# Second attention: other TensorE work behind the odd units, unread products beside the transposes

## The reference

```python
def _L1_xattn_ref(q, k, v, gamma):
    B, Dq, Lq = q.shape            # 32, 64, 256
    h = N_HEAD                     # 8 heads of 8 rows each
    qh = q.reshape(B, h, dq, Lq)
    kh = k.reshape(B, h, dq, Lk)
    vh = v.reshape(B, h, dv, Lk)
    qk = jnp.einsum('bhdq,bhdl->bhql', qh, kh) * scale
    sm = jax.nn.softmax(qk, axis=-1)
    ret = jnp.einsum('bhql,bhdl->bhdq', sm, vh)
    return gamma * ret.reshape(B, Dv, Lq)

x = x + jnp.tanh(g_xattn[1]) * _L1_xattn_ref(_layernorm(x, axis=-1), ctx_2048, ctx_2048, L1_xattn_gamma)
```

## Time and profile before

| | |
|---|---|
| median of 3 runs | 708.63 us (707.4 to 709.66) |
| the profiled execution's own time | 710.47 us |
| its span, first to last instruction | 708.7 us |
| TensorE busy, whole span | 626.2 us (88%) |
| VectorE, ScalarE, POOL busy | 501.0, 422.5, 283.4 us |
| mean granted clock of TensorE | 0.942 |

### The profile page before, as it was taken

The page is one execution under the profiler, slowest core; times in us unless marked ns, Lnnn a source line. Parts: engine busy times, 40 slices in busy tenths (PEclk is TensorE's granted clock), DMA queues, the critical chain, the costliest instruction groups (busy, mean ns, idle before and its releaser), DMA issues. The chain is left out here.

```text
span 708.7 us, 16712 instructions
## 1 busy us (share of the span) xinstructions
PE 626.2 (88%) x5047; PEld 456.8 (64%) x5047; DVE 501.0 (71%) x885; ACT 422.5 (60%) x859; POOL 283.4 (40%) x385
## 2 busy tenths in 40 slices
PE   3788869999999758999999999999859889999995
PEld 2676747788888655444444444444457779999874
DVE  3878784788887965788888888788427744444656
ACT  3888864434343513888888888888825325555430
POOL 2455544222223453444434443453243624214254
PEclk9999987999999965999999999999959979999998
DMA  5444449000000043344333443342000236546444
GB/s 157 113 111 127 132 141 324 19 1 1 0 0 21 4 137 107 96 114 129 112 104 107 122 118 108 101 120 60 2 0 33 93 103 193 162 128 193 120 135 126
DMA packets 70369, 70.42 MB, mean 99 GB/s; under 512 B 10420, under 2 KB 66580, under 8 KB 70324
## 3 DMA queue, kind: packets, MB, share of 16 engines
q1 hardware_dynamic: 65092, 55.55, 26.7%
q0 software_dynamic: 5232, 14.29, 6.7%
HBM read 38.22 MB, written 31.33 MB: 98 GB/s over the span
## 5 line engine op out<-in xcount | busy, mean ns | idle before, releaser
L1375 DVE TENSOR_REDUCE a_smax<-a_s 128x4 f32<-128x1024 f32 x128 | 153.7, 1208 | 38.9 <-PE a_s L1307 37.6
L1189 ACT ACTIVATE a_prob<-a_st 128x512 f32<-128x512 f32 x256 | 144.1, 596 | 38.8 <-PE a_st L1302 37.5
L1302 PEld LDWEIGHTS a_st<-qop,kop 25*128 25x128 f32 x512 | 60.9, 185 | 71.3 <-issue 54.8
L1307 PE MATMUL a_s<-kop,qop 24*128 24x256 f32 x512 | 99.9, 339 | 7.4 <-DVE a_smax L1375 5.0
L1302 PE MATMUL a_st<-qop,kop 25*128 25x256 f32 x512 | 100.3, 330 | 6.6 <-ACT a_prob L1189 5.7
L1246 PE MATMUL a_pv<-a_prob,a_vt 128*32 128x256 f32 x1024 | 81.6, 391 | 2.2 <-ACT a_pv_sb L1174 0.7
L806 POOL TENSOR_TENSOR f_hs_lo<-f_kept,f_hs_hi 128x512 fp32r<-128x512 f32 x32 | 41.3, 1323 | 89.1 <-ACT f_hs_hi L756 89.1
L1307 PEld LDWEIGHTS a_s<-kop,qop 24*128 24x128 f32 x512 | 60.3, 190 | 9.8 <-DVE a_smax L1375 6.3
L1820 POOL DMA_INDIRECT sorted_rows<-m_xn,m_slot x32 | 32.9, 1029 | 49.5 <-PE m_gu L126 26.7
L124 PE MATMUL f_bank<-f_xt_hi,w_hi 128*128 128x512 f32 x128 | 51.6, 403 | 1.1 <-DVE w_raw L849 0.6
L125 PE MATMUL f_bank<-f_xt_lo,w_hi 128*128 128x512 f32 x128 | 50.8, 397 | 0.0
(11 more groups left out here) (260 smaller groups left out, 1700.7 us busy)
## 6 DMA issues: line engine op xcount, KB each, us to landing
kop<-kop_rows SPq DMA_DIRECT2D x128, 48.0 KB
qop<-qop_rows SPq DMA_DIRECT2D x128, 48.0 KB
sorted_rows<-x_all SPq DMA_DIRECT2D x2, 2944.0 KB, 15.4
expert_rows<-turned SPq DMA_DIRECT2D x46, 128.0 KB
kop_rows<-k_hi SPq DMA_DIRECT2D x32, 128.0 KB, 2.3
qop_rows<-q_hi POOLq DMA_DIRECT2D x30, 128.0 KB, 2.4
qop<-sorted_rows SPq DMA_DIRECT2D x24, 128.0 KB, 2.2
kop<-sorted_rows SPq DMA_DIRECT2D x22, 128.0 KB, 2.5
```

The source lines that it names most:

```text
L1189: act.activation(prob[:, u % 8], st_ps[u % 2][:], ACT.Exp, scale=SCALE1).then_inc(prob_ready, 1)
L1302: st = pe.matmul(st_ps[u % 2][:, c * D:(c + 1) * D], lhsT=kop[t.slot][strip, u // 4, c * P:(c + 1) * P], rhs=qop[t.slot][strip, u // 4], s ...
L1307: sm = pe.matmul(s_ps[j % 2][:, k, c * D:(c + 1) * D], lhsT=qop[v.slot][strip, w // 4, c * P:(c + 1) * P], rhs=kop[v.slot][strip, w // 4], ...
L1375: dve.tensor_reduce(smax[:, v.slot, opposite(2 * j):opposite(2 * j) + 2].rearrange("p u q -> p (u q)"), s_ps[j % 2][:].rearrange("p u (q n ...
```

## The change

It does three things in TensorE's program, and nothing in the others'. The unread products of 512 columns before units 0, 4, 8 and 12 go. In their place two of 256 columns each, into columns 256 to 511 of `misc`, stand before each of the three sets of transposes, behind the waits of these. And what stood behind an even unit moves behind an odd one: `turn` for tile t from unit 2 to unit 1, both selection batches from units 6 and 8 to unit 7, and the transposes of the context from unit 14 to unit 13. In each place the weighted products of that unit come first.

```diff
-                def spare(u):
-
-                    pe.matmul(s_ps[j % 2][:, 0], lhsT=kop[v.slot][:, u // 4, 0:P],
-                              rhs=kop[v.slot][:, u // 8 * 2:u // 8 * 2 + 2].rearrange("p g n -> p (g n)"), start=True, stop=True)
+                def spare(count=2):
+
+                    if v.inside(TILES) and t.inside(TILES):
+                        for g in range(count):
+                            pe.matmul(misc[:, D:2 * D], lhsT=kop[v.slot][:, g % 2, 0:P], rhs=kop[v.slot][:, g % 2], start=True, stop=True)
...
-                    if v.inside(TILES) and t.inside(TILES) and u % EVERY == 0:
-                        spare(u)
...
-                    if u == 2:
-                        turn(t, 1, lambda: after(pe, vt_ready, t))
                     if u in (1, 3):
                         products(o, 3, u // 2)
+                    if u == 1:
+                        def before():
+                            after(pe, vt_ready, t)
+                            spare()
+                        turn(t, 1, before)
                     if u % 2 and u > 3:
                         products(t, u // 4 - 1, u % 4 // 2)
-                    if u in (6, 8):
-                        selected(o, u // 2 - 3)
+                    if u == 7:
+                        for m in range(2):
+                            selected(o, m)
                     if u == 11:
                         def before():
                             after(pe, neg_t_ready, t, 2)
                             after(pe, back_ready, o)
+                            spare()
                         turn(v, 0, before)
-                    if u == 14 and v.inside(TILES):
+                    if u == 13 and v.inside(TILES):
 
                         after_dma(pe, ctx_loaded, v)
                         after(pe, neg_t_ready, v, 2, 1)
                         if v.known and v.n == 0:
                             pe.wait_ge(vt_cleared, 2)
+                        spare()
                         for c in range(DC):
                             mm = pe.transpose(misc[:, c * P:(c + 1) * P], ctx_t[:, v.slot, c * P:(c + 1) * P], ident[:])
                         mm.then_inc(vt_done, 1)
```

More of the change, by code:

```diff
@@ L1003, in attention1 @@
         FILL = 18
-        EVERY = 4
         FIRST = Step(0, 0, 1)
```

## The result

The changed kernel takes 714.37 us (median of 10, 708.33 to 715.68) against 708.17 us for the kernel before (median of 10). The ratio is 1.0061, with a 95% interval of 1.0036 to 1.0086. The ten fall in two groups: four at 708.3 to 710.2 us with a mean clock of 0.933 to 0.937, and six at 714.1 to 715.7 us with 0.922 to 0.926. The profiled execution is of the upper group. It took 714.64 us, with a span of 712.9 us against 708.7, and a mean clock of 0.925 against 0.942. The forecast was 716.1 us. The total came out near it, but not for the reason that I gave, as the profile shows at once.

The account below looks back on a forecast made before the run. TensorE was taken as nearly the bound, coupled with ScalarE and VectorE. Waiting up 2.5 us against 1.97 of work saved gave plus 0.57, taken as 0.54; 14 steps made 7.5 us on 708.63: 716.1 us, range 703 to 722.

Parts of the forecast that it names:

- What bounds the kernel: Steady step of the second attention: TensorE nearly the bound, busy 13.87 of 14.36 us, tightly coupled with ScalarE and VectorE.
- The waits of TensorE in the new step: Hand-placed steady step: TensorE waits 3.51 us, before scores 1, 5, 7, 11 and weighted products 12/13; 2.5 more than before.
- TensorE's work: Steady step: the sum of TensorE's parts falls from 13.39 to 11.42 us, 1.97 us saved.
- plus 0.57 us: Steady step: 2.5 us more waiting against 1.97 of work saved, 14.93 us instead of 14.36; taken as 0.54.
- rival 1: Steady step: the saved work comes through if TensorE waits under 2.94 us; step 13.7, time 699 us; chance 0.17.
- I take 0.43 a group: Three groups of two 256-column unread products a step: 0.43 us each, between 0.32 and 0.50, plus 1.29 us.
- Who else is moved: Turn at unit 1 waits for VectorE's negated maxima, 0.7 us of cover; SP's store of the maxima; both cost nothing.
- Which steps: Of 15 steps with unread products the first counts as zero; 14 x 0.54 = 7.5 us.
- From -1 to +1: First of the 15 steps, mostly at the low clock behind 18 warm-up products: counted as zero, within this range.
- Rival 3: Clock falls without unread products from unit 1 to 11: one 4 us stretch a step, 25 us more, 741; chance 0.08.
- The evidence against it: From 495 to 507 us there is no unread product, yet the clock stays at 1.00, with TensorE busy throughout.

Follow-up runs that it names:

- e12: The kernel before with 512-column unread products before every even unit in steps 2 and 3 and none after; ratio 0.9855 over two of its four executions.
- e3: The kernel before, placement kept, with the change's unread products (two of 256 columns beside each set of transposes); ratio 0.9929 over six of 12 executions.
- e9: The changed kernel plus a 512-column unread product before every even unit in steps 2 and 3; ratio 0.9971 to the kernel before.
- e10: The kernel before with the change's unread products, both selections behind unit 7, and a 512-column unread product before every even unit in steps 2 and 3; ratio 0.9956.
- e11: As e10 but without any unread products after step 3; ratio 0.9772 to the kernel before, 692.7 us.
- e8: The kernel before with the change's unread products, both selections behind unit 7, and 512-column ones before units 0, 4, 8, 12 in steps 2 and 3; ratio 0.9904.
- e5: The changed kernel itself, run once more on another chip; ratio 0.9995 to the kernel before over ten of its 12 executions.

## Why the prediction was right in number and wrong in its working

**What bounds the kernel:** right. The three engines are coupled through the two banks of transposed scores, and the odd unit's wait is what decides. The waits of TensorE in the new step were placed at 3.51 us. Read off the rows they are 1.02 before scores 1 (409.71 to 410.73), 0.90 before scores 5, 0.22 before scores 7, 0.60 before scores 11 and 0.45 before the weighted products of 12/13: 3.19 us, each in its place.

**TensorE's work:** the step that failed. I had 11.42 us; it is 14.09 - 3.19 = 10.90. Three terms were too large. The groups of unread products take 0.34 and not 0.43 (3 x 0.09 = 0.27 us). Two selections behind weighted products take 0.86 and not 1.14, as batches of the same shape follow each other more closely (0.28 us). The transposes of the context take 0.31 up to the next scores and not 0.37. These are 0.61 us; the pair 8/9, drawn apart by 0.07, takes 0.50 and not 0.43, so 0.52 us less in all (the rest is rounding). With the 0.32 us less of waiting they turn plus 0.57 us into minus 0.27 in this step (14.09 against 14.36), and minus 0.34 over the 13. The point from which rival 1 decides was rightly put as TensorE's waiting against 14.36 less its work, but with a work of 10.90 the point lies at 3.46 and not at 2.94, and the waiting of 3.19 is below it. In the step, then, rival 1 came true, to which I gave 0.17.

**"I take 0.43 a group":** the low end that I named, 0.32, was nearly right. In the trace the two weight loads of a group lie between 405.95 and 406.25 us, beside products that last from 405.95 to 406.45: the second load is hidden.

**Who else is moved:** right, cost nothing. The turn at unit 1 was not held up by VectorE (no wait at 411.73), and SP's store of the maxima wasn't waited for.

**Which steps:** wrong on the first. "From -1 to +1" was said of it; the clock falls in it, at 285.6 us, and the low stretch costs 5.4 us.

**Rival 3:** the mechanism that gave the sign. I priced it as 4 us at the low level in every step, 25 us in all, and gave it 0.08. It is one stretch of 20 us near the start, worth 5.4 us, in most executions. Its reason was half right: the light load that matters is that behind the warm-up products, not that between units 1 and 11 of a steady step, where the clock held in both executions of the changed kernel that were profiled. The evidence against it said nothing of the start. Nor is a busy TensorE a guard in the steady part: in e12 it was busy for 25.73 of 26.29 us, and 5 us later the clock fell.

The Trainium skill, in "TensorE: Matmul & The Clock Gate", Part 4 (PE-mode transpose), says that transposes don't count as activity in the way products do. The runs don't decide it: in e3, e9 and e10 the clock held with the unread products beside the transposes, in e11 with none.

So the total of 716.1 us was near 714.4 by luck, by two errors that cancelled. Over the steady steps I had 7.5 us more, and 4.4 us less came: 11.9 us too much. And I had at zero the 5.4 us of the low stretch, the 1.3 and 3.5 us at and behind the end of the stage, and the 1.6 us gained ahead of the steady part: 8.6 us too little.

## What to carry to other kernels

Where two engines pass buffers to and fro, mending a pair that TensorE can run at once doesn't pay by itself. Ask how long the half has waited behind which the work is put, and what the other engine has left to do meanwhile: the selections, behind unit 7, which waited 0.22 us, gained 0.2 us a step; the turn and the context transposes, the first of them behind unit 1, which waited 1.02 us, together lost 0.5. That the length of the wait makes the difference is my reading of the rows; it wasn't tried by itself. Price a batch by the row that stands in the same company, since a second product of the same shape costs less than the first alone. And look at the granted clock of every stretch and of every execution before you believe a median: unread products may be best spent just behind the warm-up, but taking out the later ones is a bet on the clock.

## What the runs showed of the hardware that I had not expected

- The low level can persist under full load. TensorE was busy 15.92 of 16 us at 0.50 in the changed kernel, 25.00 of 25 in e8, and 39.93 of 40 in e12, where it stayed low for some 245 us. The Trainium skill, "TensorE: Matmul & The Clock Gate", Part 1 (What's actually happening), lets sustained activity release the throttle; these rows don't agree with that, if a busy TensorE in the profile is what is meant by activity, and the measurement decides.
- Two full-array products of 256 columns in a row took 0.34 us up to what followed, one of 512 columns 0.43; eight-instruction batches behind one another took 1.43 us for three and 0.57 for one alone.
- The same light stretch lets the clock fall in one execution and not in the next (e5: 8 of 12 with a lowered mean clock; e8: 5 of 12). In e3, 6 of 12 had it lowered further, to 0.886 to 0.917; where in the span isn't known.
